# An LSTM cell's state, its tanh and its scan inputs moved from PSUM to SBUF, in a deformable convolution, attention and LSTM kernel

## The reference

```
i_t = sigmoid(xi_t + h @ V_i)
g_t = tanh(xg_t + h @ V_c)
o_t = sigmoid(xo_t + h @ V_o)
c_new = h * c + i_t * g_t
h_new = o_t * tanh(c_new)
```

## Time and profile before

| what | value |
|---|---|
| median of 3 runs | 424.03 us (423.84 to 425.36) |
| the profiled execution | 425.57 us |
| its span, first to last instruction | 423.8 us |
| busy in the span | PE 399.5 us, DVE 240.2, ACT 262.9, POOL 59.3 |
| granted PE clock, mean over the span | 0.994 |
| first write of H, last write of H | 109.4 us, 421.1 us |

### The profile page before, as it was taken

How to read it: one execution, slowest core, us unless ns; L and a number is a source line. 1 busy time by engine, 2 the same in 40 slices (tenths; PEclk the granted TensorE clock), 3 DMA queues, 4 the chain that set the end, 5 groups by cost and what they waited for, 6 DMA issues and landing times.

```text
span 423.8 us, 14792 instructions
## 1 busy us (share of the span) xinstructions
PE 399.5 (94%) x5669; PEld 215.5 (51%) x5669; DVE 240.2 (57%) x1161; ACT 262.9 (62%) x1127; POOL 59.3 (14%) x131
## 2 busy tenths in 40 slices
PE   8999998888999899999999999999899999999996
PEld 2555553545455455545555554555455545554332
DVE  2477745154565566656565656665566656565443
ACT  1676643563786587568748865876587568744443
POOL 6000004001111111012111102111111012110000
PEclk9999998999999999999999999999999999999999
DMA  7000000000000000000000000000000000000000
GB/s 243 0 2 2 2 2 0 0 2 2 3 3 2 4 6 2 4 2 5 5 2 5 4 2 4 5 3 3 2 6 3 2 2 7 3 3 5 2 2 5
DMA packets 2244, 3.78 MB, mean 9 GB/s; under 512 B 1277, under 2 KB 1726, under 8 KB 2174
## 3 DMA queue, kind: packets, MB, share of 16 engines
q1 hardware_dynamic: 1872, 2.32, 1.8%
q10 hardware_dynamic: 302, 0.52, 0.4%
HBM read 2.57 MB, written 0.26 MB: 7 GB/s over the span
## 4 chain that ended last, share of the span: by engine, by line
PE 69%; DVE 12%; ACT 12%; issue 5%; DMA 1%; POOL 1%; DVEq 0%
PE bank L349 20%; PE bank L620 15%; PE bank L478 7%; DVE bank L1036 5%; PE bank L416 5%; PE bank L404 5%; PE bank L489 4%; DVE H L1046 4%; ACT bank L760 4%; PE bank L506 3%; ACT bank L753 3%; PE bank L377 2%; ACT E L734 2%; ACT QB L726 2%; PE bank L518 1%
## 5 line engine op out<-in xcount | busy, mean ns | idle before, releaser
L349 PE MATMUL bank<-FB 128*128 128x512 bf16 (+3 forms) x677 | 184.4, 369 | 1.2 <-DVE FB L786 1.2
L620 PEld LDWEIGHTS bank<-H,VW 128*32 128x32 f32 x3072 | 53.0, 109 | 92.9 <-DVE H L1046 88.1
L620 PE MATMUL bank<-H,VW 128*32 128x4 f32 x3072 | 75.6, 179 | 12.6 <-DVE H L1046 5.6
L1036 DVE TENSOR_TENSOR_SCAN bank<-bank,SU 64x12 f32<-64x12 f32 x256 | 48.7, 190 | 64.9 <-ACT bank L753 62.2
L753 ACT ACTIVATE bank<-bank 64x8 f32<-64x8 f32 x256 | 37.9, 148 | 73.1 <-PE bank L620 72.1
L1046 DVE SCALAR_TENSOR_TENSOR H<-TO,bank 64x4 f32<-64x4 f32 x256 | 40.9, 160 | 49.2 <-ACT bank L760 47.4
L349 PEld LDWEIGHTS bank<-FB 128*128 128x128 bf16 x677 | 50.9, 99 | 31.4 <-issue 5.7
L760 ACT ACTIVATE bank<-bank 64x4 f32<-64x4 f32 x256 | 38.8, 152 | 17.6 <-DVE bank L1036 2.9
L757 ACT ACTIVATE TO<-bank 64x4 f32<-64x4 f32 x256 | 44.1, 172 | 6.3
L1030 DVE SCALAR_TENSOR_TENSOR SU<-H,bank 64x4 f32<-64x4 f32 x256 | 41.4, 162 | 9.0
L333 POOL TENSOR_SCALAR E<-E,rinv 128x256 f32<-128x256 f32 x56 | 27.0, 481 | 139.5 <-DVE rinv L909 139.5
(11 more groups left out here) (117 smaller groups left out, 341.1 us busy)
## 6 DMA issues: line engine op xcount, KB each, us to landing
AW<-in_attn_w SPq DMA_DIRECT2D x1, 768.5 KB, 8.1
DW<-in_dcn_w SPq DMA_DIRECT2D x1, 576.0 KB, 6.7
X<-in_x_fm SPq DMA_DIRECT2D x1, 256.0 KB, 3.3
X<-in_x_fm ACTq DMA_DIRECT2D x1, 256.0 KB, 5.2
out_dram<-OUT SPq DMA_DIRECT2D x8, 32.0 KB, 1.4
CW<-in_conv_w SPq DMA_DIRECT2D x1, 243.5 KB, 4.2
VEC<-in_vecs SPq DMA_DIRECT2D x1, 160.0 KB, 8.0
K<-in_consts ACTq DMA_DIRECT2D x1, 154.0 KB, 3.6
```

The lines of the kernel that those rows point to most:

```text
L349: nc.tensor.matmul(idle[:, 0:n], FB[:, 0:P], FB[:, 0:n], start=True, stop=True)
L620: mm = nc.tensor.matmul(gate_out(m, gate, r, slice(B * s, B * (s + 1))), VW[:, gate, r], H[:, (STEPS * m + s - 1) % RING, :], start=False, ...
L1036: nc.vector.tensor_tensor_scan(CS.rearrange("p b q -> p (b q)"), GT.rearrange("p b q -> p (b q)"), SU[:].rearrange("p b q -> p (b q)"), 0. ...
```

## The change

- IG and CST are new SBUF tiles. CS (the state, now four places per image) and TC (its tanh) are views of partitions 64 to 127 of CST; GT and SU are gone.
- gate_out: i goes to partitions 0 to 63 and c to 64 to 127 of the same columns of the cell bank, o to partitions 0 to 63 of bank b_cs. One tanh over 128 partitions writes both into IG in SBUF, each value twice. u goes into IG's partitions 64 to 127.
- The scan takes 15 elements, its two inputs from IG's lower and upper partitions, and writes CS in SBUF.
- VW and H enter gate_sums with 64 rows in place of 128.
- preload waits ahead of the o gate for the last tanh of o of the tile before.
- Filler: NS_STEP 820 to 730, NS_TABLE 900 to 620.
- Offsets: LEAD 33, NARROW one earlier, and of the norms' steps all but the first two later by one or more; the sum at NARROWED, the statistics of the third norm, its aggregate and its last step change sides between beside_gates and beside_tanh. With LEAD at 33 offset o of tile m falls on step o - 1 of tile m-1.

The diff, without the three places where a wait for zeroed goes from 9 to 10:

```diff
--- before.py
+++ after.py
@@ -53,15 +53,15 @@
 PROJECTED = 21
 WIDEN = 22
 GELU = 23
-NARROW = 25
+NARROW = 24
 NARROWED = 26
-STATS = (22, 26, 28)
-AGGR = (23, 26, 28)
-CENTRED = (24, 27)
-SCALED = (24, 28, 29)
-CELL_INPUT = 30
-CELL_READY = 31
-LEAD = 32
+STATS = (22, 27, 29)
+AGGR = (23, 27, 30)
+CENTRED = (25, 28)
+SCALED = (26, 29, 31)
+CELL_INPUT = 31
+CELL_READY = 32
+LEAD = 33
 OUT_LAG = 1
 GN_EPS = LN_EPS = 1e-5
@@ -70,9 +70,9 @@
 COLS_LN = 5632
 COLS_TURN = 256
 COLS_TURNED = 2048
-NS_STEP = 820
+NS_STEP = 730
 NS_FILL = 54
-NS_TABLE = 900
+NS_TABLE = 620
 MOST = 3 * 512
 COLS_EARLY = 512
@@ -179,7 +179,8 @@
         H = sb("H", [P, RING, B])
-        SU = sb("SU", [C, B, 3])
+        IG = sb("IG", [P, B, 4])
+        CST = sb("CST", [P, 5 * B])
         TO = sb("TO", [C, B])
         OUT = sb("OUT", [P, 2, C])
         FB = sb("FB", [P, 512], BF16)
@@ -198,9 +199,9 @@
         b_v = [b_t, b_c0, b_c1, b_pv]
         rsum = [b_s[i][:, N:N + 1] for i in range(2)]
-        CS = b_cs[C:P, 0:3 * B].rearrange("p (b q) -> p b q", q=3)
-        TC = b_cs[C:P, 3 * B:4 * B]
-        GT = b_cs[0:C, 0:3 * B].rearrange("p (b q) -> p b q", q=3)
+        CS = CST[C:P, 0:4 * B].rearrange("p (b q) -> p b q", q=4)
+        TC = CST[C:P, 4 * B:5 * B]
+        ig = IG[:].rearrange("p b q -> p (b q)")
         ld_x, ld_x1, ld_cw, ld_dw, ld_aw, ld_lw, ld_k, ld_v, zeroed, fb_zero, cs_zero = (sem(n) for n in (
@@ -262,8 +263,9 @@
         def gate_out(m, gate, rows, cols):
-            half, place = ((0, 0), (0, P), (C, 0))[gate]
-            return b_cell[m % 2][half + rows.start:half + rows.stop, place + cols.start:place + cols.stop]
+            half, place = ((0, 0), (C, 0), (0, P * (m % 2)))[gate]
+            return (b_cell[m % 2], b_cell[m % 2], b_cs)[gate][half + rows.start:half + rows.stop,
+                                                              place + cols.start:place + cols.stop]
         @block.sync
         def _(sp):
@@ -291,7 +293,8 @@
             nc.gpsimd.memset(H[:], 0.0).then_inc(zeroed, 1)
             nc.gpsimd.memset(VW[:], 0.0).then_inc(zeroed, 1)
             nc.gpsimd.memset(XT[:], 1.0).then_inc(zeroed, 1)
-            nc.gpsimd.memset(SU[:], 1.0).then_inc(zeroed, 1)
+            nc.gpsimd.memset(IG[:, :, 0:3], 0.0).then_inc(zeroed, 1)
+            nc.gpsimd.memset(IG[:, :, 3], 1.0).then_inc(zeroed, 1)
             nc.gpsimd.memset(YF[:], 0.0).then_inc(zeroed, 1)
             nc.gpsimd.memset(AY[:], 0.0).then_inc(zeroed, 1)
             nc.gpsimd.memset(QB[:], 0.0).then_inc(zeroed, 1)
@@ -564,10 +567,12 @@
                 else:
                     pe.wait_ge(v_sb, B)
                     pe.wait_ge(lw_done, 6)
-                    pe.wait_ge(zeroed, 9)
+                    pe.wait_ge(zeroed, 10)
                 for gate in range(3):
+                    if gate == 2 and m >= 1:
+                        pe.wait_ge(o_gate, STEPS * m)
                     nc.tensor.matmul(gate_out(m, gate, slice(0, C), slice(0, P)), UW[:, gate, :],
-                                     XT[:, m, :, :].rearrange("p s b -> p (s b)"), start=(gate != 1), stop=True,
+                                     XT[:, m, :, :].rearrange("p s b -> p (s b)"), start=True, stop=True,
                                      skip_group_check=True)
             def switched(g):
@@ -617,8 +622,8 @@
             def gate_sums(m, s, gate):
                 for r in (slice(0, HC), slice(HC, C)):
-                    mm = nc.tensor.matmul(gate_out(m, gate, r, slice(B * s, B * (s + 1))), VW[:, gate, r],
-                                          H[:, (STEPS * m + s - 1) % RING, :], start=False, stop=True,
+                    mm = nc.tensor.matmul(gate_out(m, gate, r, slice(B * s, B * (s + 1))), VW[0:C, gate, r],
+                                          H[0:C, (STEPS * m + s - 1) % RING, :], start=False, stop=True,
                                           skip_group_check=True)
                 return mm
@@ -745,13 +750,13 @@
                 act.wait_ge(h_mm, 2 * m + 1)
                 nc.scalar.activation(GE[:].rearrange("p j q -> p (j q)"), b_t[:, 0:FT * P], ACT.Gelu).then_inc(ge_done, 1)
-            act.wait_ge(zeroed, 9)
+            act.wait_ge(zeroed, 10)
             for g in EVERY:
                 if 0 <= g < LAST:
                     m, s = divmod(g, STEPS)
                     act.wait_ge(ig_mm, g + 1)
-                    nc.scalar.activation(GT[:, :, 1:3].rearrange("p b g -> p g b"),
-                                         b_cell[m % 2][0:C, 0:2 * P].rearrange("p (g s b) -> p g s b", g=2, b=B)[:, :, s, :],
+                    nc.scalar.activation(IG[:, :, 0:3:2],
+                                         b_cell[m % 2][:, B * s:B * (s + 1), None].to_broadcast([P, B, 2]),
                                          ACT.Tanh).then_inc(gates, 1)
                     act.wait_ge(o_mm, g + 1)
                     nc.scalar.activation(TO[:], gate_out(m, 2, slice(0, C), slice(B * s, B * (s + 1))), ACT.Tanh
@@ -952,9 +957,7 @@
                     if m == 0 and o in VALUES_OUT_AT[:2]:
                         values_out(VALUES_OUT_AT.index(o))
                     if m == 0 and o == VALUES_OUT_AT[-1] + 3:
-                        dve.wait_ge(v_sb, B)
                         nc.vector.memset(CS, 0.0).then_inc(cs_zero, 1)
-                        nc.vector.memset(GT[:, :, 0], 0.0).then_inc(cs_zero, 1)
                     if o in EXP_AT:
                         largest(m, EXP_AT.index(o))
                     if o in HEADS:
@@ -977,20 +980,17 @@
                         dve.wait_ge(h_mm, 2 * m + 2)
                         nc.vector.tensor_tensor(FF[:].rearrange("p j q -> p (j q)"), b_pv[:, 0:FT * P],
                                                 GE[:].rearrange("p j q -> p (j q)"), ALU.mult).then_inc(ff_done, 1)
-                    if o == NARROWED:
-                        dve.wait_ge(ff_mm, m + 1)
-                        dve.wait_ge(x1_done, m + 1)
-                        nc.vector.tensor_tensor(R2[:], b_t[:, 0:C], X1[:], ALU.add).then_inc(r_done, 1)
                     if o == STATS[1]:
                         dve.wait_ge(r_done, 2 * m + 2)
                         norm_stats(m, 1, R2[:])
+                    if o == AGGR[2]:
+                        norm_aggr(m, 2)
                     if o == CENTRED[1]:
                         centre(m, 1, R2[:], VEC_G2)
                     if o == SCALED[1]:
                         scale(m, 1, T1[:, m, :], R2[:], TB[:, m, :]).then_inc(t1_done, 1)
-                    if o == STATS[2]:
-                        dve.wait_ge(t1_done, m + 1)
-                        norm_stats(m, 2, T1[:, m, :])
+                    if o == SCALED[2]:
+                        norm_apply(m, 2, LN3[:], T1[:, m, :]).then_inc(ln3_done, 1)
                     if o == CELL_READY:
                         dve.wait_ge(xt_mm, m + 1)
                         nc.vector.tensor_copy(XT[0:C, m, :, :].rearrange("p t b -> p (t b)"), b_t[0:C, 0:P]
@@ -1015,10 +1015,13 @@
                         norm_stats(m, 0, R1[:])
                     if o == AGGR[1]:
                         norm_aggr(m, 1)
-                    if o == AGGR[2]:
-                        norm_aggr(m, 2)
-                    if o == SCALED[2]:
-                        norm_apply(m, 2, LN3[:], T1[:, m, :]).then_inc(ln3_done, 1)
+                    if o == NARROWED:
+                        dve.wait_ge(ff_mm, m + 1)
+                        dve.wait_ge(x1_done, m + 1)
+                        nc.vector.tensor_tensor(R2[:], b_t[:, 0:C], X1[:], ALU.add).then_inc(r_done, 1)
+                    if o == STATS[2]:
+                        dve.wait_ge(t1_done, m + 1)
+                        norm_stats(m, 2, T1[:, m, :])
             for g in EVERY:
                 cell_step = 0 <= g < LAST
@@ -1026,16 +1029,15 @@
                     if g >= 1:
                         dve.wait_ge(h_done, g)
                     else:
-                        dve.wait_ge(cs_zero, 2)
-                    nc.vector.scalar_tensor_tensor(out=SU[:, :, 2], in0=H[0:C, (g - 1) % RING, :], scalar=0.5,
+                        dve.wait_ge(cs_zero, 1)
+                    nc.vector.scalar_tensor_tensor(out=IG[C:P, :, 1], in0=H[0:C, (g - 1) % RING, :], scalar=0.5,
                                                    in1=CS[:, :, 2], op0=ALU.mult, op1=ALU.mult).then_inc(u_done, 1)
                 beside_gates(g)
                 if cell_step:
                     dve.wait_ge(gates, g + 1)
                     dve.wait_ge(u_done, g + 1)
-                    nc.vector.tensor_tensor_scan(CS.rearrange("p b q -> p (b q)"),
-                                                 GT.rearrange("p b q -> p (b q)"),
-                                                 SU[:].rearrange("p b q -> p (b q)"), 0.0,
+                    nc.vector.tensor_tensor_scan(CS.rearrange("p b q -> p (b q)")[:, 0:4 * B - 1],
+                                                 ig[0:C, 1:4 * B], ig[C:P, 0:4 * B - 1], 0.0,
```

(2 more changed lines are left out.)

## The result

The changed kernel takes 467.09 us (median of 4 runs, 464.05 to 472.46) against 424.49 before, a ratio of 1.098 (95% interval 1.092 to 1.104). I had forecast 444.0 with a range of 418 to 450: the sign was right, and the time is outside the range. The run of 472.46 counts as slow, as it is over 1.5% above the fastest, and is left out of the ratio. The profiled execution takes 464.05 us with a span of 462.2 and a mean granted clock of 0.926; the other three runs have 0.898 to 0.923.

A forecast was written before the change was run, and what follows sets the result against it. The kernel was taken as bound by the closed loop of each cell step, 1.15 us. Loop +12.0, collision +11.2 and offsets, table steps and start -2.8 gave +20.4 us, so 444 us, range 418 to 450.

The forecast's parts named there:

- The loop: Closed chain of gates, tanh, scan, tanh and H in each cell step: +47 ns a step, times 256, +12.0 us.
- fourth rival: PE's clock falls to 1.2 GHz in the softmax steps as filler thins: 466 us, chance 0.04.
- Less filler in the ordinary steps is worth nothing: Thinner filler in ordinary cell steps gains no time, because PE is seen waiting for H there.
- The collision: In softmax steps of tiles 1 to 7, H on DVE waits for POOL's product: 0.2 us times 56, +11.2 us.
- it has some 0.38 us: Slack of u on DVE between H and the scan, so that waiting for POOL costs u nothing.
- The offsets: New placing of operations among steps; with the table steps, -0.97 + 0.5 = -0.47 us a tile, times 7, -3.3 us.
- the products with U beside the scores: Both PE works now share one step and must finish before the next gates: some +0.3 us a tile.
- The table steps: Steps behind the gelu and Exp tables get shorter through less filler and earlier queries: 0.28 and 0.25 us a tile.
- The +0.5 ahead of the first step: One more filler and the earlier queries delay the first product by some +0.5 us.
- Rival 1: No collision of DVE's H with POOL's product, the loop alone counts: 433 us, chance 0.25.
- Rival 2: Scan and H on DVE gain from leaving PSUM, up to 65 ns each, so the kernel gets faster: chance 0.18.
- Rival 3: ACT reads four elements from SBUF at no extra cost in the second tanh: +17 ns, about 425.6 us, chance 0.06.

The follow-up runs named there:

- e7: Kernel before with the changed cell alone (state, its tanh and scan inputs in SBUF, gates on 64 rows), old offsets and filler: 452.46 us, ratio 1.065.
- e6: Kernel before with the changed offsets alone (LEAD 33, norms a step apart), old filler and cell: 426.02 us, ratio 1.003.
- e3: Kernel before with the thinner filler alone (NS_STEP 730, NS_TABLE 620): 419.38 us, ratio 0.988.
- e2: Changed kernel with the gates on 128 rows again, half of them zero, a single run: 447.15 us, clock 1.00.
- e1: Changed kernel with the filler plan of before (NS_STEP 820, NS_TABLE 900): 450.08 us, ratio 1.060.
- e5: Changed kernel with the cell state and its tanh back in PSUM: 432.49 us, ratio 1.017.
- e10: Kernel before with thinner filler, norms' operations spread one to a gap within LEAD 32, and gates on 64 rows: 415.18 us, ratio 0.978.
- e11: Changed kernel with the gates on 128 rows again, four timed runs: 447.47, 453.45, 456.89 and 458.06 us, ratio 1.060.
- e9: Kernel before with SU alone moved from SBUF partitions 0 to 63 to 64 to 127: 434.46 us, ratio 1.022.
- e4: Changed kernel with POOL's product over 1 column of E instead of 256, probabilities left unscaled, a single run: 438.49 us.
- e12: Kernel before with norms' operations spread one to a gap within LEAD 32 and still thinner filler (NS_STEP 640): 431.93 us, ratio 1.015.

## Why the prediction was wrong

The parts and the whole, in us against the kernel before as timed beside each:

| kernel | change |
|---|---|
| cell alone (e7) | +27.7 |
| offsets alone (e6) | +1.2 |
| filler alone (e3) | -4.9 |
| sum of the three | +24.0 |
| all three together | +42.6 |
| all three, but gates on 128 rows, clock at 1.00 (e2) | +22.9 |

- **The loop** was right: +47 ns forecast, 1.19 for 1.15 measured. First tanh 179 for a forecast of 175, second 205 for 202, scan 185 for 193, H 157 for 160, gates 0.03 earlier.
- **The clock** was the step that failed. I had it as the fourth rival, priced it at 22 us, gave it 0.04 and left it out of the sum and the range. It costs 464.05 - 447.15 = 17 us in the profiled execution and 20 by the medians, against a miss of 23. The argument that misled me was that the clock was 1.00 with far more filler, which says nothing on how much is enough. "Less filler in the ordinary steps is worth nothing" was wrong on both sides: it is part of what costs those 17 to 20 us beside the changed cell, whose steps are longer for the same PE work, and it gives 1.7 us beside the old one (e3). e1, e3 and e5 are the proof: with the old filler, with the old cell and offsets, or with the changed kernel's steps shortened, the clock stays up in every run. Length of step decides more than rows: with 64 rows and the thinner filler all eight runs with short steps (e5, e10) stay at 0.994 or more, while with long steps 128 rows don't keep it up (e11). How much of the fall the 64 rows add isn't settled.
- **The rival's own price** came out near, 466 for 467.09, by luck. It had 0.4 us in each of 56 pairs of steps. The low clock took four stretches and not all of the softmax, cost some 0.6 to 1.1 us a pair there, and 6.5 of its 17 us are in the step behind the gelu table, four times, which the rival didn't have.
- **The collision** with POOL was right in cause and near in price (0.2 x 56 = 11.2 forecast, 0.17 x 49 = 8.3 to 8.7 measured) and wrong in place. I let H be held and u be free. H isn't held, for the reciprocal too lost its overlap with the scan and so POOL's product begins behind H. u is, and "it has some 0.38 us" is read from a bare step: in a step with a maximum that gap is full, so every ns of u is on the path.
- **The lost overlap** was missing altogether. No row that I read from gave it a price, though the trace has it: in any softmax step of the kernel before, the scan starts ahead of the end of the maximum (the first pair of rows under e9). With +0.08 to +0.11 in some 50 steps it is 4 to 5.5 us in the changed kernel, an estimate, and 9.3 by itself in the kernel before (e9), some 5.6 of it in the steps with a maximum and most of the rest in the norms'.
- **The offsets** and table steps gave -0.47 a tile in my sum; the offsets alone give +1.2 us in all. The norms' steps gained 0.33 and not 0.44, and the products with U beside the scores cost 0.53 and not 0.3. **The table steps** gave more than I said, 0.67 a tile and not 0.28 + 0.25, though the second of them only in six tiles. The +0.5 ahead of the first step isn't seen: the first H is at 108.2 us where it was at 109.4.

That the sum without the clock came so close (+20.4 against +22.9) is partly luck: the overlap I had missed on one side, and on the other the collision sized too dear and the table steps too small, nearly cancel.

Rival 1, no collision, got 0.25 and fell with the held u's of 0.34 us and with e4. Rival 2, a DVE that gains from leaving PSUM, got 0.18. Its inputs gain 3 ns at H (160 to 157), its output 16 at the scan (201 in e5, 185 after): a real gain, but far from the 65 ns for each with which the rival was worked out. Rival 3, a free source at four elements, fell to the 205 of the second tanh. How these 53 ns divide between source and destination isn't shown: the row from which I took 20 for the destination, tanh of o from PSUM to SBUF at 172 ns, is 156 in the changed kernel.

## What to carry to other kernels

Filler that only keeps the clock up can be too little (e12, the changed kernel), and how little is too little is seen in no profile of a kernel that has more: when a change makes steps longer or products smaller and takes filler away, try the filler by itself on both sides. Where small operations follow one another on DVE, look at whether one starts ahead of the other's end, and keep operands on partitions that let it go on; a slack read from a bare step isn't the slack of a crowded one. Keep what ACT reads and writes four elements at a time in PSUM (150 ns and not 205 for a tanh).

## What was unexpected

- Moving one SBUF operand of a 12-element scan from partition 0 to partition 64 costs the kernel 2.2% (e9), while maximum, scan and H keep their lengths.
- The clock's fall isn't gradual: it has its two levels, and in e12 one tile is wholly at 1.00 and the next at a mean of 0.67, with the same instructions; the runs of that kernel lie between 430.5 and 443.8 us.
- At the lower level the filler itself holds up the work that it was to protect: behind the gelu table it takes 2.00 us and not 1.09.
- The changed kernel's four runs spread over 8.4 us, where the kernel before has 1.5.
- A DVE output in PSUM costs some 16 ns at 15 elements, an input in PSUM 3 at the most.
